# Moving six small index transfers of ScalarE's queue in a two-layer graph network kernel

## The chip, the cores and the metric

One Trainium2 chip, one core. The metric is the time of one execution on the device in microseconds (us); lower is better. The kernel before was timed three times: 349.17, 349.36 and 350.13 us, median 349.36.

## The reference

x has 256 nodes by 1024 features, and src and dst are 8192 edge indices. The first layer computes logits of edges in three classes (edges 0 to 127 "hh", 128 to 767 "oo", the other 7424 "ho"), each from two node rows and its own weights, a softmax over the edges of each target, and a weighted sum of node rows; the second layer is an attention layer with one weight matrix. Each layer is followed by a residual and a layer norm.

```python
feat = concatenate([n_f[edge_src], n_f[edge_dst]], axis=1)
e_hh = relu(feat[:E_HH] @ W_hh + b_hh)
e_oo = relu(feat[E_HH:E_HH + E_OO] @ W_oo + b_oo)
e_ho = relu(feat[E_HH + E_OO:] @ W_ho + b_ho)
logit = (concatenate([e_hh, e_oo, e_ho], axis=0) @ W_a + b_a)[:, 0]
alpha = softmax of logit over the edges of each edge_dst
z_f = segment_sum(alpha[:, None] * n_f[edge_src], edge_dst)
nf2 = concatenate([n_f, z_f], axis=1)
x = layernorm(x + concatenate([relu(nf2[:64] @ W_hn + b_hn), relu(nf2[64:] @ W_on + b_on)]))
x = layernorm(x + gat(x, L1_W, L1_a, src, dst))
```

## The kernel before, in words

Each engine runs its own hand-written list of instructions in order, and semaphores tie the lists together. An instruction that waits holds up all that stands behind it on its engine.

**Work.** x is loaded in two halves of its columns (x_nat, two transfers of 512 KB), transposed by TensorE into PSUM (L1266), copied by ScalarE as a rounded part (xT_hi, L514) and completed by VectorE with the rest (xT_lo, L804). The weights come as 44 pairs of chunks of 128 rows; all but the first pair are single 1 MB transfers into four slots of W_raw. For most chunks ScalarE makes the rounded part (W_hi, `high(n)`, L505), VectorE the rest (W_lo, `low(n)`, L796), and TensorE multiplies with both (`x_dense`, L1227). Between chunks VectorE sorts the 7424 "ho" edges into tiles by class (L832 to L869). Products of the tables are later gathered for 73 tiles of edges, reduced on VectorE (L1033) and scattered; then come the softmax, the update and the second layer.

**Who sends what.** SyncE's queue carries, in order, x's first half, the first chunk of W_oo (L363), x's second half, the second chunk (L365), three 1 MB pairs (L367), then the biases b_oo, W_a, b_a, b_hh and b_ho, each broadcast to 128 partitions (L370 to L374). A fourth 1 MB pair is sent once the first slot of W_raw is free, which needs low(1). ScalarE's queue carries at the very start `edges` (two transfers of 29 KB, src and dst, semaphore edges_in, 232 bytes for each partition) and the four index transfers `st_col` (0.5 and 2.5 KB each for src and dst, semaphore indices_in, 4 or 20 bytes for each partition). Only after these six issues does ScalarE wait for eps_made and run a one-column copy, which loads its function table.

**Order around the change.** ScalarE then runs: x_high(0, 2) on "xT0a", high(0), x_high(2, 4) on "xT0b", high(1), x_high(4, KC) on "xT1", high(2), high(3), and more. VectorE runs x_low "xT0a", low(0), x_low "xT0b", a wait for edges_in (L831), four small operations on the edges (L832 to L835), low(1), x_low "xT1", the class one-hots (L839), low(2), the running count (L842), low(3), and so on. TensorE warms up with ten small products of the identity (L1260), transposes blocks 0 to 1 and 2 to 3 of x's first half, runs seven more small products, transposes the second half, and starts on the chunks. GpSimd, after its constants, waits for indices_in and gathers the rows of x of the "hh" edges by two indirect transfers (x_rows, L417), which TensorE transposes ahead of chunks 6 and 7 (L1331). VectorE itself waits for indices_in only at L871. `edges` is read by L832 and L833 alone, `st_col` by L417, L430, L436 and L872.

Of the kernel before, what the change touches and what calls it, by code (L numbers as in the profile page):

```python
# [5 lines left out]
P = 128  # L6
# [4 lines left out]
E_HH, E_OO = 128, 640  # L11
E_ST = E_HH + E_OO
# [28 lines left out]
def gnn_two_layers(nc, x, src, dst, W_hh, b_hh, W_oo, b_oo, W_ho, b_ho, W_a, b_a, W_hn, b_hn, W_on, b_on,  # L41
# [6 lines left out]
    with ctx:  # L48
        def sb(name, shape, dt=F32, stack=ctx):
            return stack.enter_context(nc.sbuf_tensor(name, shape, dt))  # L50

        def sem(name):
            return ctx.enter_context(nc.semaphore(name))
# [30 lines left out]
        st_col = sb("st_col", [P, 2, 1 + JO], I32)  # L84
# [32 lines left out]
        eps_ln = sb("eps_ln", [P, 1])  # L117
        warm = sb("warm", [P, 2])
# [86 lines left out]
        def flat(T, a=0, b=KC):  # L205
            return T[:, a:b, :].rearrange("p c n -> p (c n)")
# [13 lines left out]
        x_in = [sem(f"x_in{k}") for k in range(2)]  # L220
        first_in = sem("first_in")
        edges_in = sem("edges_in")
        indices_in = sem("indices_in")
# [4 lines left out]
        eps_made = sem("eps_made")  # L228
# [45 lines left out]
        stream += [(name, W_hn if name == "hn" else W_on, k) for name, k in update_order]  # L274
        stream += [("l1", L1_W, k) for k in range(0, KC, 2)]
        chunks = [(name, k + i) for name, _, k in stream for i in range(2)]

        END = {"ooA": 8, "ooB": 16, "hoA": 30, "hh": 40, "hoB": 48, "hn": 76, "upd": 80, "h1": 88}
# [15 lines left out]
        def apart(n):  # L294

            return END["hoB"] + NB <= n < UX or END["upd"] <= n < END["upd"] + 4
# [5 lines left out]
        def in_ring(n):  # L302

            return [m for m in range(n + 1) if split(m) and not apart(m)]
# [5 lines left out]
        def halves(n):  # L310

            in_place = lo_in_raw[:, n // 2 % NS, n % 2, :]
            if late(n):
                return (hi_early[n - END["upd"]] if apart(n) else W_hi[:, ring(n), :]), in_place
            if apart(n):
                return hi_apart[n - END["hoB"] - NB], in_place
            return W_hi[:, ring(n), :], W_lo[:, ring(n), :]
# [16 lines left out]
        def pe_at(s):  # L334
            return PE_STAGES.index(s) + 1
# [150 lines left out]
        @block.scalar  # L486
        def _(act):
            sa = nc.scalar
            for k, v in enumerate((src, dst)):
                act.dma_start(edges[:, k, :], v[E_ST:E].rearrange("(p j) -> p j", p=P)).then_inc(edges_in, 16)  # L490
            for k, v in enumerate((src, dst)):
                act.dma_start(st_col[:, k, 0:1], v[0:E_HH].rearrange("(p j) -> p j", p=P)).then_inc(indices_in, 16)
                act.dma_start(st_col[:, k, 1:], v[E_HH:E_ST].rearrange("(p j) -> p j", p=P)).then_inc(indices_in, 16)
            act.wait_ge(eps_made, 1)
            sa.copy(warm[:, 0:1], eps_ln[:])

            def high(n):

                if n == 0:
                    act.wait_ge(first_in, 16)  # L500
                else:
                    act.wait_ge(w_in[n // 2 % NS], 16 * (n // 2 // NS + 1))
                if len(in_ring(n)) > NB and not apart(n):
                    act.wait_ge(chunk_used, in_ring(n)[-1 - NB] + 1)
                sa.copy(halves(n)[0], W_raw[:, n // 2 % NS, n % 2, :]).then_inc(hi_made, 1)  # L505
# [6 lines left out]
            def x_high(a, b, name):  # L512
                act.wait_ge(pe_step, pe_at(name))
                sa.copy(flat(xT_hi, a, b), G0[:, a * N:b * N]).then_inc(act_step, 1)  # L514
# [16 lines left out]
            x_high(0, 2, "xT0a")  # L531
            high(0)
            x_high(2, 4, "xT0b")
            high(1)
            x_high(4, KC, "xT1")
            high(2)
# [1041 lines left out]
```

## Time and profile before

| | |
|---|---|
| median of three timed runs | 349.36 us (349.17 to 350.13) |
| span of the profiled execution | 345.9 us |
| busy TensorE / VectorE / ScalarE / GpSimd | 325.6 / 290.3 / 195.6 / 116.4 us |
| chain that ended last | VectorE 45%, TensorE 43%, ScalarE 5%, DMA 2% |
| mean granted TensorE clock | 0.990 |

The profiled execution's own time is not listed apart from the three; its span runs from the first to the last instruction, and the median is 3.46 us above it. The profile has a page for the whole (busy shares, the chain that ended last, groups of instructions, DMA issues) and views that are asked for stretches: the chain in order of time, the timeline, one tile's instructions with the time from issue to landing of its transfers, and the DMA queues. q1 is SyncE's queue, q10 ScalarE's.

### The profile page before, as it was taken

The page shows a single profiled execution, that of the slowest core. Times are in us where ns is not written, and L with a number is a line of the kernel's source. Part 1 is how long each engine was busy: PE and PEld are TensorE (multiplying, and loading weights), DVE is VectorE, ACT ScalarE, POOL GpSimd, SP SyncE. Part 2 cuts the span into 40 slices and gives each one's busy share as a digit, 9 for nine tenths or more (in the row PEclk, how much of TensorE's full clock was granted, in tenths as well). Part 3 has the DMA queues.
Part 4 walks back from the last instruction along what each step waited for, and adds up shares of the span by engine and source line. Part 5 has one row for each costly group of instructions (what it writes and reads, how often), then busy time and mean ns, then how long its engine had stood idle before and what let it go on. Part 6 is the DMA issues. An engine that isn't in the chain of part 4 may idle for free.

```text
span 345.9 us, 4739 instructions
## 1 busy us (share of the span) xinstructions
PE 325.6 (94%) x1496; PEld 250.8 (73%) x1496; DVE 290.3 (84%) x415; ACT 195.6 (57%) x306; POOL 116.4 (34%) x128
## 2 busy tenths in 40 slices
PE   7899999999999999999999999999899999979980
PEld 7678887677644788588888888888686676758730
DVE  0999999973999979899999999988888877894545
ACT  3755396202043346588888888737149576821355
POOL 4200061084000840079999999720001200060000
PEclk9999999999999999999999999999999999999996
DMA  6999599789999996003030000023498886000003
GB/s 225 402 406 408 235 310 389 246 264 235 300 363 286 375 372 217 0 0 123 3 121 2 0 3 1 2 61 123 169 350 290 321 328 243 2 0 1 0 0 121
DMA packets 17654, 63.10 MB, mean 182 GB/s; under 512 B 2250, under 2 KB 2252, under 8 KB 17376
## 3 DMA queue, kind: packets, MB, share of 16 engines
q1 hardware_dynamic: 13536, 50.07, 39.1%
q0 software_dynamic: 2096, 8.74, 8.7%
q10 hardware_dynamic: 2000, 4.00, 3.5%
q8 instruction: 13, 0.21, 0.3%
q14 instruction: 9, 0.07, 0.1%
HBM read 59.64 MB, written 3.16 MB: 182 GB/s over the span
## 4 chain that ended last, share of the span: by engine, by line
DVE 45%; PE 43%; ACT 5%; DMA 2%; issue 2%; SPq 0%; ACTq 0%; DVEq 0%
DVE ps L1033 25%; PE ps L1227 12%; PE ps L1276 8%; DVE W_lo L796 5%; PE ps L1434 5%; PE ps L1505 4%; PE ps L1246 3%; DVE lo_in_raw L796 3%; PE ps L1442 2%; DMA W_raw<-in_L_gnn_W_oo_dram 2%; PE ps L1537 2%; PE ps L1469 2%; DVE tile_val L815 1%; PE ps L1308 1%; PE ps L1290 1%
## 5 line engine op out<-in xcount | busy, mean ns | idle before, releaser
L505 ACT CAST W_hi<-W_raw 128x1024 fp32r<-128x1024 f32 x62 | 63.0, 1045 | 58.6 <-DMA W_raw<-in_L_gnn_W_ho_dram 28.4
L1033 DVE SCALAR_TENSOR_TENSOR ps<-ps,wa_bc 128x1024 f32<-128x1024 f32 x73 | 86.4, 1261 | 1.3 <-PE ps L1392 1.3
L796 DVE TENSOR_TENSOR W_lo<-W_raw,W_hi 128x1024 fp32r<-128x1024 f32 x54 | 65.1, 1238 | 10.3 <-ACT W_hi L505 8.3
L1392 PE MATMUL ps<-A_tab,oh 128*128 x146 | 52.1, 438 | 0.8 <-DVE ps L1033 0.8
L1227 PE MATMUL ps<-W_hi,xT_hi 128*128 128x512 f32 x112 | 45.9, 410 | 1.0 <-DVE W_lo L796 0.9
L1392 PE MATMUL ps<-B_tab,oh 128*128 x146 | 45.9, 395 | 0.0
L1227 PE MATMUL ps<-W_lo,xT_hi 128*128 128x512 f32 x112 | 43.7, 390 | 0.0
L1227 PE MATMUL ps<-W_hi,xT_lo 128*128 128x512 f32 x112 | 34.6, 390 | 0.0
L454 POOL TENSOR_SCALAR sc<-sc 128x256 f32<-128x256 f32 x37 | 32.6, 882 | 3.2
L452 POOL TENSOR_TENSOR sc<-irow,keys 128x256 f32<-128x256 f32 x37 | 23.7, 641 | 26.5 <-PE ps L1399 26.0
L1392 PEld LDWEIGHTS ps<-B_tab,oh 128*128 128x128 f32 x146 | 27.4, 188 | 6.2 <-issue 0.5
L1399 PEld LDWEIGHTS ps<-sc 128*128 128x128 f32 x146 | 27.1, 188 | 6.2
L611 ACT ACTIVATE sc<-sc,keys 128x64 f32<-128x64 f32 x73 | 23.7, 340 | 13.5 <-DVE ps L1033 13.1
L1276 PE MATMUL ps<-W_raw,hh_x 128*128 128x512 f32 x64 | 28.2, 593 | 0.0
L1227 PEld LDWEIGHTS ps<-W_hi,xT_hi 128*128 128x128 f32 x112 | 21.0, 188 | 7.5 <-issue 2.0
L598 ACT ACTIVATE oh_dist<-key_rows,pcol 128x512 bf16<-128x512 uint8 x37 | 26.2, 707 | 0.0
L605 ACT ACTIVATE oh<-oh_dist 128x512 fp32r<-128x512 bf16 x37 | 23.2, 627 | 4.5 <-PE ps L1392 4.3
L1227 PEld LDWEIGHTS ps<-W_lo,xT_hi 128*128 128x128 f32 x112 | 21.1, 188 | 4.6 <-issue 0.7
L1392 PEld LDWEIGHTS ps<-A_tab,oh 128*128 128x128 f32 x146 | 22.7, 189 | 2.3 <-issue 2.0
L1227 PEld LDWEIGHTS ps<-W_hi,xT_lo 128*128 128x128 f32 x112 | 21.0, 188 | 4.6
L1399 PE MATMUL ps<-sc 128*128 128x64 f32 x146 | 23.9, 247 | 0.0
L1276 PEld LDWEIGHTS ps<-W_raw,hh_x 128*128 128x128 f32 x64 | 11.9, 190 | 13.5 <-issue 13.4
(283 smaller groups left out, 585.4 us busy)
## 6 DMA issues: line engine op xcount, KB each, us to landing
W_raw<-in_L_gnn_W_ho_dram SPq DMA_DIRECT2D x8, 1024.0 KB, 5.2
W_raw<-in_L_gnn_W_hh_dram SPq DMA_DIRECT2D x8, 1024.0 KB, 8.6
W_raw<-in_L_gnn_W_hn_dram SPq DMA_DIRECT2D x8, 1024.0 KB, 4.8
W_raw<-in_L_gnn_W_on_dram SPq DMA_DIRECT2D x8, 1024.0 KB, 5.2
W_raw<-in_L_gnn_W_oo_dram SPq DMA_DIRECT2D x7, 1024.0 KB, 12.2
W_raw<-in_L_gnn_W_dram SPq DMA_DIRECT2D x4, 1024.0 KB, 4.9
key_rows<-key_rows_scratch POOLq DMA_DIRECT2D x1, 2304.0 KB, 13.8
table_scratch<-tabs ACTq DMA_DIRECT2D x2, 1024.0 KB, 6.4
```

Of the source, the lines that this page charges most:

```text
L452: link(ga.tensor_tensor(pair, irow[:, 1:Q + 1].unsqueeze(1).unsqueeze(1).broadcast_to([P, 2, 2, Q]), keys[:, t:t + 2, 0:2].unsqueeze(3).br ...
L454: ga.tensor_scalar(pair, pair, 0.0, None, ALU.is_equal).then_inc(ends_made, 1)
L505: sa.copy(halves(n)[0], W_raw[:, n // 2 % NS, n % 2, :]).then_inc(hi_made, 1)
L598: sa.activation(oh_dist[:, j % 2, :, :], key_rows[:, :, 2 * j * P:2 * (j + 1) * P], ACT.Abs, bias=pcol[:, 1:2]).then_inc(dist_made, 1)
L605: sa.activation(oh[:, j % 2, :, :], oh_dist[:, j % 2, :, :], ACT.Relu, bias=1.0, scale=-1.0) \
L611: sa.activation(sc[:, t % U, 2, :], sc[:, t % U, 1, :], ACT.Copy, scale=keys[:, t, 2:3]) \
L796: v.tensor_tensor(lo, W_raw[:, n // 2 % NS, n % 2, :], hi.bitcast(F32), ALU.subtract).then_inc(lo_made, 1)
L1033: v.scalar_tensor_tensor(acc, acc, 0.0, wa_bc[:], ALU.max, ALU.mult, accum_out=keys[:, t, 2:3]).then_inc(reduced, 1)
L1227: ins = mm(acc[:, m * D + f:m * D + f + 512], x_part(n - first, m), W[:, f:f + 512], start=(n == first and x_part is hi and W is W1), stop ...
L1276: ins = mm(G0[:, f:f + 512], hh_x[:, row // KC, row % KC, :], W_raw[:, n // 2 % NS, n % 2, f:f + 512], start=(row == 0), stop=(row == 2 * ...
L1392: ins = mm(acc[:, n * 512:(n + 1) * 512], oh[:, t // 2 % 2, k, t % 2 * P:(t % 2 + 1) * P], tab[:].rearrange("p q d -> p (q d)")[:, n * 512 ...
L1399: ins = mm(G0[:, bass.ds(column.with_bounds(min_val=0, max_val=15 * Q), Q)], sc[:, t % U, 1:3, :].rearrange("p r n -> p (r n)"), sc[:, t % ...
```

## The change

ScalarE's one-column copy comes first. Then ScalarE waits until x's first half has landed (x_in[0]) and sends the two `edges` transfers. The four `st_col` transfers are sent after x_high(2, 4), ahead of high(1). Nothing else differs.

```diff
             sa = nc.scalar
+            act.wait_ge(eps_made, 1)
+            sa.copy(warm[:, 0:1], eps_ln[:])
+            act.wait_ge(x_in[0], 16)
             for k, v in enumerate((src, dst)):
                 act.dma_start(edges[:, k, :], v[E_ST:E].rearrange("(p j) -> p j", p=P)).then_inc(edges_in, 16)
-            for k, v in enumerate((src, dst)):
-                act.dma_start(st_col[:, k, 0:1], v[0:E_HH].rearrange("(p j) -> p j", p=P)).then_inc(indices_in, 16)
-                act.dma_start(st_col[:, k, 1:], v[E_HH:E_ST].rearrange("(p j) -> p j", p=P)).then_inc(indices_in, 16)
-            act.wait_ge(eps_made, 1)
-            sa.copy(warm[:, 0:1], eps_ln[:])
...
             x_high(0, 2, "xT0a")
             high(0)
             x_high(2, 4, "xT0b")
+            for k, v in enumerate((src, dst)):
+                act.dma_start(st_col[:, k, 0:1], v[0:E_HH].rearrange("(p j) -> p j", p=P)).then_inc(indices_in, 16)
+                act.dma_start(st_col[:, k, 1:], v[E_HH:E_ST].rearrange("(p j) -> p j", p=P)).then_inc(indices_in, 16)
             high(1)
             x_high(4, KC, "xT1")
```

## Rows read from the trace of the kernel before

**Rows 1.** The chain that ended last, 2 to 53 us: start us, us, what.

```profile
2.27 8.22 DMA W_raw<-in_L_gnn_W_oo_dram
10.52 1.06 ACT W_hi L505
...
11.68 1.23 DVE W_lo L796
...
52.33 11.46 PE ps L1227 x48
```

**Rows 2.** Timeline, issues of ScalarE's queue (start us, us, engine, line, what).

```profile
0.82 0.45 ACTq L490 DMA_DIRECT2D edges<-in_src_dram  x1
1.29 0.49 ACTq L490 DMA_DIRECT2D edges<-in_dst_dram  x1
1.81 0.45 ACTq L492 DMA_DIRECT2D st_col<-in_src_dram  x1
...
3.58 0.59 ACTq L493 DMA_DIRECT2D st_col<-in_dst_dram  x1
```

**Rows 3.** Timeline, issues of SyncE's queue.

```profile
0.81 0.43 SPq L350 DMA_DIRECT2D x_nat<-in_x_dram  x1
...
5.97 1.61 SPq L372 DMA_DIRECT2D ba_bc<-in_L_gnn_b_a_dram  x1
7.63 1.37 SPq L374 DMA_DIRECT2D bias_bc<-in_L_gnn_b_hh_dram  x1
9.04 1.47 SPq L374 DMA_DIRECT2D b_ho_bc<-in_L_gnn_b_ho_dram  x1
...
34.07 0.37 SPq L367 DMA_DIRECT2D W_raw<-in_L_gnn_W_ho_dram  x1
```

**Rows 4.** Timeline, ScalarE's first copies.

```profile
6.77 0.58 ACT L514 CAST xT_hi<-ps 128x512 fp32r<-128x512 f32 x1 [1.08 <-PE ps L1266]
7.49 1.04 ACT L505 CAST W_hi<-W_raw 128x1024 fp32r<-128x1024 f32 x1
8.44 0.58 ACT L514 CAST xT_hi<-ps 128x512 fp32r<-128x512 f32 x1
...
13.22 2.00 ACT L505 CAST W_hi<-W_raw 128x1024 fp32r<-128x1024 f32 x2 [0.74 <-DMA W_raw<-in_L_gnn_W_oo_dram]
```

**Rows 5.** Timeline, TensorE's warm-up and first transposes.

```profile
1.63 3.89 PE L1260 MATMUL ps<-ident 128*128 128x128 f32 x20 [1.63 <-POOL ident L396]
...
6.08 1.09 PE L1266 MATMUL ps<-ident,x_nat 128*128 128x128 f32 x8 [0.56 <-DMA x_nat<-in_x_dram]
```

**Rows 6.** Timeline, VectorE around its wait for the edges.

```profile
9.71 0.68 DVE L804 TENSOR_TENSOR xT_lo<-ps,xT_hi 128x512 fp32r<-128x512 f32 x1
...
10.54 0.23 DVE L832 TENSOR_SCALAR e_i<-edges 128x116 int32<-128x116 int32 x1
```

**Rows 7.** DMA issues by line: what, queue, count, KB each, us from issue to landing.

```profile
edges<-in_src_dram ACTq DMA_DIRECT2D x1, 29.0 KB, 4.4
edges<-in_dst_dram ACTq DMA_DIRECT2D x1, 29.0 KB, 6.4
...
st_col<-in_dst_dram ACTq DMA_DIRECT2D x1, 2.5 KB, 9.8
```

**Rows 8.** Tile x_nat: landing of its two transfers, first and second half.

```profile
DMA to landing us min/median/max: 5.2/6.1/7.0
```

**Rows 9.** DMA queues from 10 to 11 us: packets, MB, share of 16 engines.

```profile
q1 hardware_dynamic: 99, 0.40, 100.1%
q10 hardware_dynamic: 97, 0.00, 5.3%
```

**Rows 10.** Gather of the "hh" rows: GpSimd's issue, TensorE's use, landing times.

```profile
13.68 1.25 POOL L417 DMA_INDIRECT x_rows<-in_x_dram,st_col  x1 [8.74 <-DMA st_col<-in_dst_dram]
...
28.43 1.91 PE L1331 MATMUL ps<-ident,x_rows 128*128 128x128 f32 x16
...
DMA to landing us min/median/max: 8.0/8.1/8.2
```

## The prediction

> **What bounds the kernel now.** I read the chain that ended last in order of time, because the change touches only the first 12 us. Until 10.52 us the chain is a transfer: W_oo's second chunk, issued at 2.27 us and landed 8.22 us later, then ScalarE's rounding of it, then VectorE's low(1) at 11.68 us [rows 1]. From there the chain runs through VectorE's sort and low parts almost without a gap, and at 52.33 us it passes to TensorE. So the start of low(1) is the number to forecast: VectorE has no idle time behind it that could take up a delay, and TensorE's products wait for its results. I carry a shift of low(1) to the end at its full size.
>
> Two routes lead to low(1), and they ended almost together. One is high(1) on ScalarE, 10.52 plus 1.06, or 11.58 us [rows 1]. The other is VectorE itself: x_low "xT0b" ends at 9.71 + 0.68 = 10.39, the first edge operation starts at 10.54, and low(1) at 11.68 [rows 6, 1]. So low(1) starts 1.14 us after the edges can be read. The edges now cost nothing: they landed at 0.82 + 4.4 = 5.2 and 1.29 + 6.4 = 7.7 us [rows 2, 7], 2.8 us ahead of their use. The change takes this cover away on one route and puts four issues ahead of high(1) on the other.
>
> **Part 1, x's first half without the six small transfers beside it.** It lands at 0.81 + 5.2 = 6.0 us [rows 3, 8] and TensorE's transposes start at 6.08 [rows 5]. Those can't start before the warm-up ends at 1.63 + 3.89 = 5.52 us [rows 5], so at most 0.5 us is won. At least nothing is won. I take 5.6 us for the landing, nearly the whole gain, since both queues' issues and packets ran together in that stretch. The table load moves forward to idle time and costs nothing; if it didn't, it would lie behind the wait for x, which nobody reads before 5.6 us.
>
> **Part 2, two issues ahead of x_high "xT0a".** ScalarE issued them in 0.45 and 0.49 us [rows 2], together 0.94. TensorE gave x_high its input 0.69 us after its own start (6.08 to 6.77) [rows 5, 4], so even at these prices ScalarE arrives at 5.6 + 0.94 = 6.54 us, 0.2 us earlier than the 6.77 of before. But what else is issuing then matters. SyncE's last issues took 1.61, 1.37 and 1.47 us, back to back from 5.97 to 10.51, where one alone later takes 0.37 [rows 3]. They wait for room in a full queue. ScalarE's six were over by 3.58 + 0.59 = 4.17 us [rows 2], before that began; now they fall in the middle of it. No row shows a ScalarE issue beside a stalled SyncE issue. The bounds are 0 (the queues are independent) and two stalls, 2 x 1.42 = 2.8 us (1.42 is the mean of 1.37 and 1.47). Between them I take one stall, 1.42 us: even ahead of the full queue the issues of both engines took 0.45 to 0.59, not 0.37 [rows 2, 3], so they share something. x_high "xT0a" then starts at 5.6 + 0.94 + 1.42 = 7.96 us, 1.2 later than before.
>
> The Trainium skill, Perfetto Trace Analysis, section "DMA Instruction — HWDGE (DVE, Sync)", says that a sequencer locks the descriptor generator for itself while it makes descriptors, and that the profiled duration of an issue includes the wait for that lock. By that rule the stall is passed on (one or two stalls, low(1) late by 1.4 us or more); if the stalled issue didn't hold the lock, this term would be 0. The trace here shows only the slight mutual slowing.
>
> **Part 3, four issues ahead of high(1).** From x_high "xT0a" to the end of x_high "xT0b" ScalarE needs 8.44 + 0.58 - 6.77 = 2.25 us [rows 4], so it ends at 10.2 us. The four index issues took from 1.81 to 4.17, 2.36 us [rows 2]; at the 0.45 of the quickest they are 1.8, at SyncE's lone 0.37 [rows 3] they are 1.5. SyncE's stalls are over by about then, so I take 1.8: 12.0 us. high(1) itself needs its chunk, at 10.5 us or earlier, which no longer binds. It ends at 12.0 + 1.06 = 13.1 us, so low(1) starts 13.1 - 11.68 = 1.4 us late. This is what queues behind the issues: high(1), x_high "xT1" and high(2). The last sat idle for 0.74 us until its data came [rows 4]; 1.5 us less 0.74 makes it 0.8 late, less than the 1.4 by which VectorE then runs late anyway, so it adds nothing of its own.
>
> **Part 4, the edges.** The second transfer starts to issue at about 5.6 + 0.45 + 1.42 = 7.5 us. Its landing time is bounded by the two of before, 4.4 and 6.4 us [rows 7]. In this case it stands alone, its predecessor being 1.9 us ahead, so 4.4 is the nearer: 11.9 us, and low(1) could start at 13.0. Both routes thus give about 13.1. With 6.4 it is 13.9 + 1.14 = 15.0 us, 3.4 late, which is the upper bound of the case.
>
> **Part 5, the index transfers' landing.** The last landed 9.8 us after issue [rows 7], at 13.4 us; the first gather is issued at 13.68, two in all take 8.2 us to land, and TensorE uses them at 28.43 [rows 10]. Each engine serves both queues in turn: 99 large packets beside 97 small ones in one microsecond, with SyncE still busy for all of it [rows 9], so small packets cost little but each waits its turn of about 16/99 = 0.16 us. Four transfers are some 36 turns, 5.8 us. Issued until 12.0, they land near 18.4. The second gather, about 1.6 us behind the first, would land at 28.2, against a use that itself has moved to 29.8. Hidden, with 1.6 us left; without that cover the chunks behind would wait for the rest. W_raw's large transfers meet the same number of small packets, only later, and I cost that at nothing; the cover is high(2), whose use on VectorE moves by 1.4.
>
> **Sum.** x_high "xT0a" moves by -0.4 (landing 5.6 for 6.0) + 0.94 + 1.42, less the 0.77 us from 6.0 to 6.77 in which ScalarE stood waiting for it: +1.2. The four issues add 1.8, and the 1.50 us for which ScalarE stood waiting for its chunk (9.02 to 10.52) [rows 4, 1] are taken up: high(1) is 1.5 late. Low(1) started 0.1 behind its end before (11.58 to 11.68), which falls away: +1.4 us. The span goes from 345.9 to 347.3 us. The median of the runs stands 3.46 above the span, so 350.8 us.
>
> **Rivals.**
> - *The queues are independent* (part 2's stall is 0). ScalarE: 6.54 + 2.25 + 2.36 + 1.06 = 12.2, or 11.7 with the cheaper issues. The edges: issued at 6.05, landed after 4.4 to 6.4 at 10.5 to 12.5, low(1) at 11.6 to 13.6, middle 12.6. Late by 0.9: 350.3 us. For it speaks that landed packets of both queues take turns without loss; against it, the slower issues. It decides by the edges: beyond a landing of 6.2 us after issue the loss passes 0.3%.
> - *Not slower.* x's first half lands at 5.3 us, as its issues and packets have the queues to themselves, the edges land within 4.4 us, and each issue takes 0.37. x_high "xT0a" starts at 5.52 + 0.69 = 6.2, its walk ends at 8.5, four issues end at 10.0, high(1) at 11.1 if its chunk is there by 10.0; the edges land at 5.67 + 4.4 = 10.1 and allow 11.2. Low(1) is 0.5 us early: 348.9 us. It decides where ScalarE is free again ahead of 10.52. It needs three good turns at once, and nothing in the walk allows more, unless a later stretch gains by itself.
> - *The gather is late.* If the index transfers land 3 us beyond my 18.4, TensorE waits 1.4 us for x_rows beyond the shift: 352.2 us.
>
> **How the numbers follow.** 0.3%, 1.05 us here, is about what a measurement of this kernel can tell from no change. Chances: the stall is passed on, 0.45 (slower 0.38, within 0.07); independent queues, 0.33 (within 0.24, slower 0.09); not slower, 0.15 (within 0.07, faster 0.08 with the unforeseen); gather late, 0.07 (slower 0.05, within 0.02). Together slower 0.52, within 0.3% 0.40, faster 0.08. The range leaves out the stronger half of the not-slower case and the double stall with slow edges (+3.4): 349.2 to 352.1. The likeliest case by itself is 350.3 to 352.7.
>
> **What would show it.** Issues of `edges` by ScalarE start near 5.6 us; one of them takes over 1 us if the stall is passed on, and both about 0.45 if not. x_high "xT0a" near 8.0 (else 6.5), high(1) near 12.0 (else 10.9), low(1) near 13.1. VectorE's wait ahead of L832 ends on the edges' transfer. TensorE passes its L1331 without a wait on x_rows. From low(1) on all should be shifted alike up to 52 us. I am wrong if low(1) is late and the end isn't, if x's first half lands where it did, or if low(1) is early.

## The result, and the profile after

The changed kernel takes 351.48 us (median of 6, 350.20 to 352.99), the kernel before 349.32 in the runs beside it: ratio 1.0070, 95% interval 1.0044 to 1.0096, so 2.2 us slower. The forecast was 350.8 with a range of 349.2 to 352.1. A second series, with 10 executions, gave 351.90 and 1.0073 (1.0049 to 1.0097). The profiled execution is the fastest of the first six, 350.20 us with a span of 347.7, which is 1.8 us above the span before. Both profiles are of the shorter executions of their kernel; what sets the longer ones apart is shown further down.

ScalarE's timeline after (columns as in [rows 2, 4]):

```profile
5.27 0.40 ACTq L493 DMA_DIRECT2D edges<-in_src_dram  x1
5.71 0.50 ACTq L493 DMA_DIRECT2D edges<-in_dst_dram  x1
6.91 0.59 ACT L512 CAST xT_hi<-ps 128x512 fp32r<-128x512 f32 x1 [4.61 <-PE ps L1267]
7.35 0.33 ACTq L533 DMA_DIRECT2D st_col<-in_src_dram  x1
...
8.34 0.59 ACT L512 CAST xT_hi<-ps 128x512 fp32r<-128x512 f32 x1
8.76 0.47 ACTq L534 DMA_DIRECT2D st_col<-in_dst_dram  x1
9.28 1.05 ACT L503 CAST W_hi<-W_raw 128x1024 fp32r<-128x1024 f32 x1 [0.35 <-DMA W_raw<-in_L_gnn_W_oo_dram]
```

Read the starts, not the program order. The four index issues begin at 7.35 us, ahead of high(0) and of x_high "xT0b" at 8.34, which stand before them in the program: they run beside the copies. ScalarE is never late for high(1). high(1) starts at 9.28 us, 1.24 earlier than in [rows 1], and waits only for its chunk. x's first half landed 4.4 us after its issue instead of 5.2 [rows 8].

VectorE's timeline after, around the edges, against [rows 6]:

```profile
9.61 0.68 DVE L805 TENSOR_TENSOR xT_lo<-ps,xT_hi 128x512 fp32r<-128x512 f32 x1
12.51 0.22 DVE L833 TENSOR_SCALAR e_i<-edges 128x116 int32<-128x116 int32 x1 [2.21 <-DMA edges<-in_dst_dram]
...
13.52 1.22 DVE L797 TENSOR_TENSOR W_lo<-W_raw,W_hi 128x1024 fp32r<-128x1024 f32 x1
```

This is the first wait that the change makes: VectorE is ready at 10.3 us and stands idle for 2.21 us until the second edge transfer lands. low(1) starts at 13.52 us, 1.84 later than before.

The chain that ended last, 8 to 66 us, after (start us, us, what):

```profile
8.76 9.49 DMA st_col<-in_dst_dram
...
18.55 2.92 POOL x_rows L417
...
21.77 9.07 DMA x_rows<-in_x_dram,st_col
...
30.89 1.97 PE ps L1332 x16
32.86 32.74 PE ps L1228 x144
```

This is the second wait. The last index transfer lands at 18.2 us instead of 13.4, GpSimd's gathers follow, and the second lands at 30.84. TensorE's row for these transposes reads, against 28.43 with no wait in [rows 10]:

```profile
30.89 1.97 PE L1332 MATMUL ps<-ident,x_rows 128*128 128x128 f32 x16 [0.46 <-DMA x_rows<-in_x_dram,st_col]
```

The wait is only 0.46 us because TensorE was itself late through the first one: it was ready at 30.43 us, 2.0 later than before. The chain names the gather, since it ended last by that much; VectorE's delay does not appear in it at all. From one profile one can't tell whether the edges, the gather or both cost the 1.8 us. I use one point to compare stages, the first permutation product behind the first 18 chunks: 63.63 us before, 65.45 after, +1.82, the whole difference of the spans.

### The profile page after: what moved, and what is told of

It reads as the page before. It is cut to its first block, busy times and chain, and to the rows that moved or that the text cites. A ratio compares the mean times of both kernels' runs of the same rounds, so it can differ in the third digit from the quotient of the medians.

```text
span 347.7 us, 4739 instructions
## 1 busy us (share of the span) xinstructions
PE 326.0 (94%) x1496; PEld 252.4 (73%) x1496; DVE 290.3 (83%) x415; ACT 195.7 (56%) x306; POOL 118.6 (34%) x128
## 4 chain that ended last, share of the span: by engine, by line
PE 51%; DVE 35%; DMA 5%; ACT 4%; issue 2%; POOL 1%; ACTq 0%; DVEq 0%; POOLq 0%
DVE ps L1034 25%; PE ps L1228 17%; PE ps L1277 8%; PE ps L1435 5%; PE ps L1506 4%; PE ps L1247 3%; DMA st_col<-in_dst_dram 3%; DVE lo_in_raw L797 3%; DMA x_rows<-in_x_dram,st_col 3%; PE ps L1443 2%; PE ps L1538 2%; PE ps L1470 2%; DVE W_lo L797 2%; PE ps L1261 1%; PE ps L1309 1%
## 5 line engine op out<-in xcount | busy, mean ns | idle before, releaser
L612 ACT ACTIVATE sc<-sc,keys 128x64 f32<-128x64 f32 x73 | 23.8, 341 | 13.8 <-DVE ps L1034 13.6
L1277 PE MATMUL ps<-W_raw,hh_x 128*128 128x512 f32 x64 | 28.2, 594 | 0.0
L1393 PEld LDWEIGHTS ps<-A_tab,oh 128*128 128x128 f32 x146 | 23.4, 188 | 2.2 <-issue 1.9
L1277 PEld LDWEIGHTS ps<-W_raw,hh_x 128*128 128x128 f32 x64 | 11.9, 190 | 13.5 <-issue 13.4
```

The lines of the kernel that those rows point to most:

```text
L612: sa.activation(sc[:, t % U, 2, :], sc[:, t % U, 1, :], ACT.Copy, scale=keys[:, t, 2:3]) \
L1277: ins = mm(G0[:, f:f + 512], hh_x[:, row // KC, row % KC, :], W_raw[:, n // 2 % NS, n % 2, f:f + 512], start=(row == 0), stop=(row == 2 * ...
L1393: ins = mm(acc[:, n * 512:(n + 1) * 512], oh[:, t // 2 % 2, k, t % 2 * P:(t % 2 + 1) * P], tab[:].rearrange("p q d -> p (q d)")[:, n * 512 ...
```

## The experiments

All edits are against the changed kernel. "Shift" is the start of that product less 63.63. Waits, low(1) and shift are of the one profiled execution of each run; the time and the ratio are of all of them.

| run | time, us | ratio to before (95%) | wait for edges / for x_rows | low(1) | shift |
|---|---|---|---|---|---|
| changed kernel | 351.48 | 1.0070 (1.0044 to 1.0096) | 2.21 / 0.46 | 13.52 | 1.82 |
| e1: edges at the start | 350.83 | 1.0066 (1.0035 to 1.0096) | 0 / 2.76 | 11.71 | 3.90 |
| e2: index at the start | 352.86 | 1.0118 (1.0093 to 1.0143) | 3.85 / 0 | 15.13 | 3.45 |
| e4: low(1) ahead of the edges | 352.27 | 1.0100 (1.0066 to 1.0135) | 0.17 / 2.94 | 10.61 | 2.37 |
| e5: e2 and e4 | 350.20 | 1.0031 (1.0011 to 1.0052) | 0 / 0 | 11.96 | 1.34 |
| e6: biases sent later | 352.06 | 1.0094 (1.0065 to 1.0122) | 2.79 / 1.3 | 14.08 | 3.25 |
| e7: edges at the start, index at x | 349.75 | 1.0024 (1.0001 to 1.0046) | 0 / 0 | 11.98 | 0.34 |
| e8: e7, edge operations first | 350.26 | 1.0048 (1.0025 to 1.0072) | 0 / 0 | 12.16 | 0.69 |
| e9: short queue | 351.59 | one execution, no ratio | 1.65 / 1.8 | 12.50 | 2.14 |
| e10: x_rows transposed later | 351.71 | 1.0067 (1.0043 to 1.0092) | 3.56 / 0 | 14.35 | 3.13 |
| e11: both waits covered | 349.46 | 1.0000 (0.9982 to 1.0018) | 0 / 0 | 10.69 | 0.17 |
| e12: e1, x_rows later | 349.46 | 1.0009 (0.9995 to 1.0024) | 0 / 0 | 11.71 | 0.12 |
| e13: changed kernel again | 351.90 | 1.0073 (1.0049 to 1.0097) | 3.07 / 0.92 | 13.78 | 2.51 |

The wait for x_rows is that of the transposes' products. In e7, e8 and e12 only the weight load ahead of them waits, for 0.5, 0.3 and 0.5 us: there the gather lands just in time.

**Each half alone (e1, e2).**

```diff
 # e1: ahead of the warm-up copy, without the wait for x
+            for k, v in enumerate((src, dst)):
+                act.dma_start(edges[:, k, :], ...)
             act.wait_ge(eps_made, 1)
             sa.copy(warm[:, 0:1], eps_ln[:])
-            act.wait_ge(x_in[0], 16)
-            for k, v in enumerate((src, dst)):
-                act.dma_start(edges[:, k, :], ...)
```

```diff
 # e2: the four st_col transfers at the start instead of behind x_high(2, 4)
+            for k, v in enumerate((src, dst)):
+                act.dma_start(st_col[:, k, 0:1], ...)
+                act.dma_start(st_col[:, k, 1:], ...)
             act.wait_ge(eps_made, 1)
...
             x_high(2, 4, "xT0b")
-            for k, v in enumerate((src, dst)):
-                act.dma_start(st_col[:, k, 0:1], ...)
-                act.dma_start(st_col[:, k, 1:], ...)
```

> Edges are sent at the start again, as in the kernel before; only the four index transfers stay behind x_high xT0b. Theory E (VectorE's wait for the edges is what sets the end): low(1) back at 11.7 us or a little earlier, time 349.3 (ratio to before 1.000). Theory G (the late gather of x_rows is enough by itself): the gather lands near 30.5 us again, TensorE would be ready for it at 28.3 and waits 2 us or more, time about 351.4 (1.006). If both are needed, something between.

> The four index transfers are sent at the start, the edges only once x's first half has landed. Theory E: VectorE waits 1.5 to 2.2 us for the edges, low(1) at 13.0 to 13.5, time 351.1 (1.005). Theory G: the gather lands before 28.4 us and nobody waits for it, time 349.3 (1.000).

Theory E (only VectorE's wait counts) and theory G (only the gather counts) both fail: both runs are slower than the kernel before. e1 keeps only the late index transfers, has low(1) where it was, and loses all the same, 1.5 us in the median (its profiled execution is the slowest of seven, with the transposes at the lower clock, as shown further down):

```profile
31.40 3.62 PE L1331 MATMUL ps<-ident,x_rows 128*128 128x128 f32 x16 [2.76 <-DMA x_rows<-in_x_dram,st_col]
```

e2 keeps only the late edges and loses more than the changed kernel. The edges, issued at 5.65 and 6.01 us, stand behind the index transfers on ScalarE's queue, for which GpSimd waits until 10.58, and the second lands 8.1 us after its issue:

```profile
14.11 0.22 DVE L833 TENSOR_SCALAR e_i<-edges 128x116 int32<-128x116 int32 x1 [3.85 <-DMA edges<-in_dst_dram]
```

low(1) is 3.45 us late there and the shift is 3.45: VectorE's delay is carried on at full size. The gather's is not. From the start of the transposes of x_rows to the point of comparison TensorE takes 35.20 us in the kernel before, 35.19 in e2 and 35.22 in e5, but 34.49 to 34.56 in the changed kernel, e4, e6, e9 and e13, where it has waited for x_rows: it regains 0.64 to 0.71 us of such a delay. So each route gives a shift of its own, and the larger one counts: low(1)'s delay on VectorE, or the delay of the transposes on TensorE less some 0.65. In the changed kernel they are 1.84 and 1.8, as good as equal; in e6 they are 2.40 and 3.3, in e13 2.10 and 2.5, in e9 0.82 and 2.2, and the gather sets the end.

**Cover the edges' wait (e4, e5).** VectorE takes low(1) and x_low "xT1" ahead of the edges.

```diff
             x_low(2, 4, "xT0b")
+            low(1)
+            x_low(4, KC, "xT1")
             dve.wait_ge(edges_in, 32)
             ...
-            low(1)
-            x_low(4, KC, "xT1")
```

> The changed kernel, but VectorE does low(1) and x_low xT1 ahead of its wait for the edges. Theory E: low(1) at 10.4 us, the edges' four operations after 12.8, the class one-hots at 14.0 us against 14.2 before and 16.0 changed, time 349.1 (0.9995). Theory G: VectorE is early but TensorE waits about 2.4 us for x_rows, time 351.4 (1.006).

> As the run before, with the index transfers sent at the start. Both theories: neither wait is left, the class one-hots at 14.0 us, time 349.1, 0 to 0.3 us below the kernel before. If it is slower than that by over 1 us, a third cost is at work.

e4: VectorE's class one-hots start at 14.16 us (14.19 before), its delay is gone, and the time doesn't fall, since TensorE is now ready for the gather at 28.57 us and waits 2.94 us for it. The two waits overlap in the changed kernel: taking one away uncovers the other. e5 was expected at 349.1 and came at 350.2. With the index transfers at the start W_oo's second chunk comes late again, high(1) starts at 10.88 us, and VectorE stands idle for 1.47 us ahead of low(1), the gap that the edge operations fill in the kernel before; now they come behind low(1) and the one-hots start at 15.49, 1.3 us late, which is the shift. So the kernel before has the better place for these operations when high(1) is late, and e4 when it is early.

**Cover the gather, then both (e10, e11, e12).** TensorE transposes x_rows one chunk later.

```diff
-            x_dense(3, 6, G1, 0, END["ooA"])
+            x_dense(3, 7, G1, 0, END["ooA"])
             pe.wait_ge(x_rows_in, 32)
...
-            x_dense(6, END["ooA"], G1, 0, END["ooA"])
+            x_dense(7, END["ooA"], G1, 0, END["ooA"])
```

> The changed kernel, but TensorE transposes x_rows one chunk (2.7 us) later, so that the late gather has landed by then. What is left is VectorE's wait for the edges. If both waits are enough by themselves: no wait for x_rows, low(1) still near 13.5, time 351.1, about as the changed kernel. If the gather alone was what set the end: 349.3.

> The changed kernel with both waits covered: VectorE does low(1) and x_low xT1 ahead of the wait for the edges, and TensorE transposes x_rows one chunk later. The transfers are as in the changed kernel. Both waits as the whole cause: class one-hots at 14.1 us as before (14.2), no wait for x_rows, time 349.1 to 349.4. If it stays above 350.4, a third cost is in the change.

> Edges at the start and the index transfers late, with x_rows transposed one chunk later. Theory: the wait of 2.8 us for x_rows that the same kernel had without this goes away, and so does its loss: time 349.1 to 349.4. If the loss stays, the late index transfers cost through something else.

With the gather covered and the edges' wait left, the loss stays (351.71). With the edges early and the gather covered, it is gone (349.46, against 350.83 without the cover). With every transfer where the change puts it and both waits covered, the ratio is 1.0000: the same six transfers at the same late times cost nothing that the runs can tell (0.9982 to 1.0018). Timelines of e11, VectorE and TensorE:

```profile
13.20 0.22 DVE L835 TENSOR_SCALAR e_i<-edges 128x116 int32<-128x116 int32 x1
...
14.22 1.12 DVE L840 TENSOR_TENSOR cls_oh<-cls,irow 128x928 bf16<-128x928 f32 x1
```

```profile
31.20 1.91 PE L1332 MATMUL ps<-ident,x_rows 128*128 128x128 f32 x16
```

Both run with no idle time ahead of them. No third cost above 0.2%, the interval's half width, is left. One rival isn't excluded by a run: the covers were not tried on the kernel before, so they could have a gain of their own that hides such a cost. The profiles speak against it: that kernel has no wait for x_rows that a cover could remove, and e11's class one-hots start at 14.22 us against 14.19.

**A version between (e7, e8).** Edges at the start, index transfers at x's landing, ahead of x_high "xT0a"; e8 also puts the edge operations ahead of low(0).

```diff
+            for k, v in enumerate((src, dst)):
+                act.dma_start(edges[:, k, :], ...)
             act.wait_ge(eps_made, 1)
             sa.copy(warm[:, 0:1], eps_ln[:])
             act.wait_ge(x_in[0], 16)
-            for k, v in enumerate((src, dst)):
-                act.dma_start(edges[:, k, :], ...)
+            for k, v in enumerate((src, dst)):
+                act.dma_start(st_col[:, k, 0:1], ...)
+                act.dma_start(st_col[:, k, 1:], ...)
...
             x_high(2, 4, "xT0b")
-            for k, v in enumerate((src, dst)):
-                act.dma_start(st_col[:, k, 0:1], ...)
-                act.dma_start(st_col[:, k, 1:], ...)
```

> Edges at the start, the four index transfers right at the landing of x's first half, 2 us earlier than in the changed kernel, ahead of x_high xT0a. With both waits of the changed kernel as causes: the index transfers land near 15.5 to 17, the gather 2 to 3 us earlier than in the run with the late index, near 28, and TensorE waits 0 to 1 us for it instead of 2.8; low(1) at 11.7. Time 349.3 to 350.0. If the late gather isn't the cause of that run's loss, the time stays near 350.8.

> As the run before, and VectorE does the four edge operations ahead of low(0), where it stood idle, instead of ahead of low(1). low(0) is 0.5 to 1 us later, low(1) starts as x_low xT0b ends, near 11.0 against 11.7, if high(1) is done by then. If the start of VectorE's chain sets the end, time 0.5 us below the run before; if the gather or the edges' landing (7.7) binds, no gain or a loss of up to 0.5.

e7: some two microseconds earlier are nearly enough for the gather, which lands just as TensorE is ready (29.01 us), and the ratio is 1.0024. Here the issues do hold ScalarE: they run from 5.54 to 7.38 us ahead of x_high "xT0a", which starts at 7.41, later than 6.77 in [rows 4]. The shift of 0.34 grows to 1.18 by 310 us in this profile; what adds to it was not followed. e8 was a miss. The same issues and the edge operations delayed low(0) to 10.19 us, and low(1) at 12.16 was no earlier (11.98 in e7). No version beat the kernel before.

**Why the edges start so late (e6, e9).** In the changed kernel the second edge transfer took 6.8 us to land, not the 4.4 of the forecast. The DMA queues from 8 to 9 us (after) show ScalarE's first packets, 2.7 to 3.7 us behind the issue at 5.27:

```profile
q1 hardware_dynamic: 114, 0.41, 100.6%
q10 hardware_dynamic: 10, 0.00, 1.1%
```

SyncE's issues were slow again at that time, at 6.53 and 7.88 us for 1.30 and 1.26 us. That they wait for room in a full queue is a reading of these numbers: one 512 KB broadcast in 1.3 us is some 400 GB/s, what the DMA engines moved in those microseconds (404 to 432). e6 takes the full queue away, e9 the packets.

```diff
 # e6
-                if n == NS - 1:
+                if n == NS:
                     sp.dma_start(bias_bc[:, 1, :], b_oo.partition_broadcast(P))...
```

```diff
 # e9
                     sp.dma_start(W_raw[:, 0, 0, :], W[0:P, :]).then_inc(first_in, 16)
+                    sp.wait_ge(x_in[0], 16)
                     x_half(1)
```

> The changed kernel, but SyncE sends its five bias and W_a broadcasts behind the fifth weight pair (near 15 us), so that its queue is never full when ScalarE sends. Theory Q (ScalarE's packets started 3 us late because SyncE's stalled issues were ahead of them): the edges land 4.4 to 5 us after issue, near 10.3, low(1) starts near 11.4, the index transfers land near 16 and the gather near 26, no wait for x_rows; time 349.0 to 349.4. Rival (the weight packets already queued on each engine cause the delay): the edges land 6 to 7 us after issue, low(1) stays near 13.5, time near 351.4.

> The changed kernel, but SyncE holds back x's second half and all that follows until x's first half has landed, so that when ScalarE sends the edges only a few packets of the first chunk are left on each DMA engine. Theory P (each engine first works off the 33 or so weight packets that it has ahead of ScalarE's): the first edge packet follows within 2.1 us of the issue, as at the kernel's start, and the edges land in 4 to 5 us. Rival (a transfer sent by ScalarE after its table load and wait takes 3.5 us to start, whatever is queued): first packet 3.5 us after issue, landing 5.8 to 7. The kernel as a whole is 2 to 4 us slower than before, because all weights come later.

e6: theory Q, that SyncE's stalled issues hold up ScalarE's packets, fails. SyncE has no slow issue left, yet the edges, issued at 5.33, have 3 packets moved by 9 us (queues from 8 to 9 us), and the second lands 7.3 us after its issue:

```profile
q1 hardware_dynamic: 111, 0.39, 97.5%
q10 hardware_dynamic: 3, 0.00, 0.3%
```

e9: with the weights held back, the first edge packets come between 6 and 7 us, under 2 us after the issue at 5.07, the two transfers land in 4.2 and 6.0 us (queues from 6 to 7 us):

```profile
q1 hardware_dynamic: 65, 0.13, 81.7%
q10 hardware_dynamic: 6, 0.00, 0.7%
```

So what stands ahead are packets that SyncE's queue already holds, not its slow issues. After the change SyncE's queue moved 137, 198 and 131 packets in the three microseconds from 5 to 8 and 114 more until 9: between the issue at 5.27 and the first edge packet that is (0.73 x 137 + 198 + 131) / 16 = 27 to 34 packets on each of 16 engines. That each engine works off the some 30 packets ahead before it turns to the other queue fits e6 too (27 to 33 by the same count); in e9 it is 3 to 7, with the first edge packet under 2 us after its issue. How many were queued was varied only in this one step. e9's landing of the second transfer, 6.0, was above the 4 to 5 expected: once started, the edges still take turns with SyncE's packets.

**The spread (e13).**

> The changed kernel once more, for its spread. Its profiled execution of before had a wait for the edges of 2.2 us and a mean granted clock of 0.990, the other executions mostly 0.981. Theory C (in those, TensorE's idle time ahead of low(1)'s product is followed by a stretch at the lower clock): if the profiled execution has a mean clock near 0.981, the granted clock is under 1.0 between 14 and 24 us and the shift at the first permutation product is 2.5 to 3.3 us instead of 1.8. If the clock is full there and lost only past 300 us, theory C is wrong for this kernel. Time 351.2 to 351.6.

The granted clock does not explain the rest of the 2.2 us, though it went to the lower level with TensorE's longer idle time. The changed kernel again (the first line: us, length, busy time of each engine, granted clock, DMA share, GB/s):

```profile
14.00:18.00 4.00, 2.94 (x7) 2.36 (x8) 3.82 (x4) 4.00 (x4) 0.00 (x0) 0.59 1.02 379
```

```profile
15.06 0.79 PE L1228 MATMUL ps<-W_hi,xT_hi 128*128 128x512 f32 x1 [2.82 <-DVE W_lo L797]
...
31.60 1.97 PE L1332 MATMUL ps<-ident,x_rows 128*128 128x128 f32 x16 [0.92 <-DMA x_rows<-in_x_dram,st_col]
```

TensorE stood idle for 2.82 us ahead of low(1)'s product, and from 14 to 18 us its granted clock was 0.59 of the full 2.4 GHz on average, between the two levels: products took 0.63 us instead of 0.39. In the first profile of the changed kernel the idle time there was 1.98 us and the clock stayed at 1.00. Yet TensorE is ready for x_rows at 31.60 - 0.92 = 30.68 us, against 30.43 in the first profile, 0.25 later, and low(1) was already 0.26 later. The lower clock used up idle time that TensorE had there anyway (0.74 us ahead of 18.56 and 0.39 ahead of 21.96 in the first profile). What makes the shift 2.51 is the gather, on which TensorE starts 0.71 us later. In e1 the lower clock did cost: it fell at the gather's wait, was 0.50 from 32 to 34 us, and the transposes took 3.62 us instead of 1.97. e1's shift is 3.90, e4's 2.37, with transposes that started within 0.11 us of each other.

A second such stretch has nothing to do with the change. Near 310 us TensorE stands idle for 2.53 to 2.55 us in all fourteen profiles. In four of them (before, after, e8, e10) the clock stays at 1.00 behind it, and from the product behind this idle time to that of L1532 (325.12 us before) it takes 15.4 us; in the other ten the clock is 0.79 or 0.80 from 310 to 318 us and it takes 16.7 to 17.0. So e11's span is 347.6 us with a shift of 0.17. The kernel before has two kinds of executions as well: of the 85 in the runs beside e1 to e13, 27 have a mean clock of 0.990 or 0.991 and a median span of 345.9 us, 58 have 0.985 to 0.987 and 347.4. That this stretch is what parts them is likely from e11 and e12, whose spans and mean clocks are those of the longer kind; no profile of a longer execution of the kernel before shows it. Of the 16 executions of the changed kernel eight had a mean clock of 0.980 to 0.982, but the three longest spans (350.4 to 350.9 us) had 0.986 or 0.987, so the mean clock doesn't rank them. The edges' wait varied with the landing: 2.21, 3.07, and 3.56 us in e10, whose code is the same up to there, and there VectorE's delay was 2.67 us and the shift 3.13.

## Why the prediction was right or wrong

**Right in its frame.** The loss of the edges' cover, the sign and the range, and that a delay of low(1) is carried to the end at its full size (3.45 to 3.45 in e2). That low(1) is the one number to forecast was not right: in e1 and e4 it is on time or early and the loss is there. Its 1.84 and the shift of 1.82 agree in the changed kernel, where the gather's route gives as much. The point, +1.4, was two thirds of the measured +2.2, and it came by terms of which several were wrong and cancelled; that is luck.

**Part 1** had x's first half at 5.6 us; it was 5.2. The gain wasn't used at the start, since TensorE's warm-up took 4.63 us, not the 3.89 that I took from before, and its transposes began at 6.05. In e13 it took 3.84, and they began at 5.35. It did move W_oo's second chunk to 9.28 us from 10.52, more than forecast.

**Part 2, the stall passed on, failed.** The likeliest case rested on it. The two edge issues were over at 6.21 us, ahead of SyncE's slow ones, and the index issues took 0.33 to 0.52 us beside those of 1.30 and 1.26 us, so the term was 0, not 1.42. The Trainium skill (Perfetto Trace Analysis, "DMA Instruction — HWDGE (DVE, Sync)") says that the generator is locked for one sequencer's use while it makes descriptors. That lock doesn't last for the whole of a slow issue by these rows: ScalarE's issue of 0.33 us, at 7.35, began and ended within SyncE's of 6.53 to 7.83. The rival with independent queues had this right for the issues.

**Part 3, four issues for 1.8 us on ScalarE, failed.** They cost 0. I treated issues as if the engine did them between its copies; the timeline shows them beside the copies, with an issue at 7.35 us ahead of a copy at 8.34 that precedes it in the program. So a copy that waits doesn't hold up the DMA issues behind it, other than the section on the kernel says of every instruction; issues do hold up a copy that stands behind them (7.41 us in e7). The Trainium skill (Advanced Engine Details and Errata, "Sequencer and Instruction Queues") says that the sequencer pushes engine instructions into a queue, where they wait for their semaphores. The trace agrees: the copy of 8.34 us must have been in such a queue when the issue of 7.35 began. Together parts 2 and 3 put high(1) at 12.0 us; it was at 9.28.

**Part 4 was the right cause with the wrong size.** The edges landed 6.8 us after issue; I took 4.4, the row of the kernel's first small transfer, sent at 0.82 us beside the very first large one (0.81), and named 6.4 as the bound. Put in the forecast's terms, the issue was set at 7.5 us for a real 5.71 and the landing at 4.4 for 6.8; the two errors left 0.6 us, which is luck too. Measured on a busy queue: 6.8, 7.0, 7.2, 7.3 and 7.5 (after, e13, e4 and e11, e6, e10). From the true issue time, 5.71 + 6.8 + 1.0 for the four operations = 13.5, which is low(1). The right rival, independent queues, said 12.6 at its middle, and its upper end, 13.6, was nearly met. It put the turning point at a landing of 6.2 us after issue; by its own issue at 6.05 us, the 1.14 and the 1.05 us of 0.3% it is 11.68 + 1.05 - 1.14 - 6.05 = 5.5. The measured 6.8 is beyond either.

**Part 5** had the landing of the indices right (18.4, measured 18.2) by luck: the last was issued at 8.76 us, not just ahead of 12.0, and took 9.5 us to land, not 6.4. It had the gather wrong (28.2, measured 30.8): GpSimd's first issue took 2.92 us instead of 1.25 and the landings 9.1 to 9.6 instead of 8.2. In other runs that issue took 1.25 to 2.48 us and the landings 7.7 to 11.9, so its size varies. I gave this rival 0.07 and priced it as something on top of the other delay. It was there beside it, and enough by itself (e1: 1.5 us in the median). That two waits overlap was in none of the cases.

**The step from span to median.** The 3.46 us were added to a span of the shorter kind of execution; the 27 of that kind have a median time of 347.81, 1.9 above their median span. The forecast is a difference, so this moved nothing.

**Not foreseen**: the lower clock behind longer idle times, which cost 1.5 us in e1's profile.

## What to carry to other kernels

Before a small transfer is moved behind a large one's landing, look at who reads it and when: an instruction in order behind its wait loses as much as the transfer is late, and a gather that hangs on it loses a second time, far away. Price the landing by a transfer that was sent into the same traffic, not by one sent at the kernel's start, and where two waits of like size appear together, cover both before judging either.

## What the hardware showed that I had not expected

A transfer sent on ScalarE's queue while SyncE's has weights in flight moved its first packet 2.7 to 3.7 us after the issue, against under 2 with few packets queued (e9), whether SyncE's issues were slow or not (e6). After that, the queues took turns one to one (94 and 94 packets from 10 to 11 us, after). DMA issues ran beside the engine's own copies (issues from 7.35 to 9.23 us, copies from 6.91 to 8.93). The length of TensorE's idle time alone doesn't decide its clock: 1.84 (e8), 2.54 (e6), 2.76 (e1), 2.82 (e13), 3.31 (e10) and 3.56 us (e2) went with a stretch at 0.50, 1.98 (after) and 2.94 us (e4) did not, and the same 2.53 to 2.55 us near 310 us did in ten profiles and did not in four. What such a stretch costs depends on the slack behind it: at most 0.1 us by TensorE's wait for x_rows in e13 and e6, where products had idle time ahead of them, and 1.5 us in e1, where they had none.
